# Second layer: four normalizations move from DVE to ACT, and POOL works out their shift

## The reference

```python
def _layernorm(x, axis=-1, eps=1e-05):
    m = jnp.mean(x, axis=axis, keepdims=True)
    v = jnp.var(x, axis=axis, keepdims=True)
    return (x - m) / jnp.sqrt(v + eps)

# _L1_xattn_ref, after the projections to 16 heads
scores = jnp.einsum('bhqd,bhkd->bhqk', q, k) * scale
attn = jax.nn.softmax(scores, axis=-1)
ctx = jnp.einsum('bhqk,bhkd->bhqd', attn, v)

x = x + _L1_xattn_ref(_layernorm(x), ctx_1024, ctx_1024, Wq, Wk, Wv, Wo)
x = x + _L1_ffn_ref(_layernorm(x), W, b, V_r, C)     # x @ W.T + b + (x @ V_r) @ C.T
```

## Time and profile before

| | us |
|---|---|
| median of three runs | 816.52 (815.5 to 820.49) |
| the profiled run | 817.38 |
| its span in the profile | 815.7 |
| busy: PE, DVE, POOL, ACT | 760.1, 474.5, 277.7, 264.3 |
| blocks 0 to 14 and the last batch | about 615 to 815.7 |

### The profile page before, as it was taken

How to read it: one execution, slowest core, us unless ns; L and a number is a source line. 1 busy time by engine, 2 the same in 40 slices (tenths; PEclk the granted TensorE clock), 3 DMA queues, 4 the chain that set the end, 5 groups by cost and what they waited for, 6 DMA issues and landing times.

```text
span 815.7 us, 14156 instructions
## 1 busy us (share of the span) xinstructions
PE 760.1 (93%) x5120; PEld 508.1 (62%) x5120; DVE 474.5 (58%) x1102; ACT 264.3 (32%) x524; POOL 277.7 (34%) x296
## 2 busy tenths in 40 slices
PE   6998999999999989989999999999989889999997
PEld 4675656755675555465666566555666666676775
DVE  2548564245734566814444473645658786888754
ACT  1323311241124121102222222222216665554562
POOL 4863615060320240611441433626693222101010
PEclk8999999999999999999999999999999999999999
DMA  9899434342250194844677654686767683662201
GB/s 257 225 307 324 123 104 131 115 133 76 87 176 15 28 375 172 278 126 125 185 201 206 194 177 140 183 251 172 214 178 203 171 224 114 182 182 71 73 2 46
DMA packets 70677, 133.53 MB, mean 164 GB/s; under 512 B 10401, under 2 KB 51362, under 8 KB 68690
## 3 DMA queue, kind: packets, MB, share of 16 engines
q1 hardware_dynamic: 54864, 81.14, 32.2%
q10 hardware_dynamic: 7906, 31.23, 13.9%
q0 software_dynamic: 7840, 20.26, 9.1%
HBM read 104.02 MB, written 28.41 MB: 162 GB/s over the span
## 4 chain that ended last, share of the span: by engine, by line
PE 74%; DVE 14%; ACT 4%; DMA 3%; issue 2%; POOL 1%; ACTq 0%; SPq 0%; DVEq 0%; POOLq 0%
PE ps L1323 14%; PE ps L1015 11%; PE ps L1339 7%; PE ps L1026 6%; PE ps L1036 4%; PE ps L2016 4%; DVE mxh L1662 4%; PE ps L2045 4%; PE ps L2036 3%; PE ps L2009 2%; PE ps L958 2%; PE ps L1330 2%; PE ps L1991 2%; PE ps L992 2%; PE ps L1046 2%
## 5 line engine op out<-in xcount | busy, mean ns | idle before, releaser
L1662 DVE TENSOR_REDUCE mxh<-ps 112x2 f32<-112x750 f32 x128 | 115.3, 934 | 22.9 <-PE ps L2016 21.5
L1323 PE MATMUL ps<-rw,rowsT 128*128 x280 | 126.1, 593 | 0.6 <-ACT rowsT L1282 0.6
L1875 ACT ACTIVATE d_pT<-ps 125x448 f32<-125x448 f32 x192 | 92.1, 548 | 66.9 <-PE ps L2036 63.5
L1015 PE MATMUL ps<-x1T,sw 128*128 128x448 f32 x256 | 102.8, 547 | 6.3 <-DVE gluT L465 4.9
L1323 PEld LDWEIGHTS ps<-rw,rowsT 128*128 128x128 f32 x280 | 50.5, 190 | 51.0 <-issue 51.0
L1015 PEld LDWEIGHTS ps<-x1T,sw 128*128 128x128 f32 x256 | 46.8, 190 | 51.7 <-issue 38.2
L2016 PE MATMUL ps<-kst,qst 96*112 96x375 bf16 x256 | 64.4, 339 | 7.8 <-DVE mxh L1662 2.8
L1339 PE MATMUL ps<-rw,gT 128*128 x280 | 66.4, 380 | 0.8 <-ACT gT L1286 0.8
L1339 PEld LDWEIGHTS ps<-rw,gT 128*128 128x128 f32 x280 | 52.9, 190 | 21.3 <-issue 15.9
L1026 PE MATMUL ps<-sw,gluT 128*112 128x256 f32 x256 | 57.8, 381 | 4.3 <-DVE gluT L465 4.3
L325 POOL DMA_INDIRECT xg<-xh_moe,places x32 | 32.8, 1024 | 83.4 <-DVE places L552 49.1
(11 more groups left out here) (239 smaller groups left out, 1257.2 us busy)
## 6 DMA issues: line engine op xcount, KB each, us to landing
rb<-in_rb SPq DMA_DIRECT2D x35, 512.0 KB, 4.3
kst<-kscr ACTq DMA_DIRECT2D x45, 378.0 KB, 5.2
rw<-in_rw SPq DMA_DIRECT2D x24, 512.0 KB, 9.9
kscr<-ka SPq DMA_DIRECT2D x16, 567.0 KB, 3.7
cT<-in_ctx_t SPq DMA_DIRECT2D x21, 378.0 KB, 5.0
ctxT<-in_ctx_t SPq DMA_DIRECT2D x16, 378.0 KB
ctxn<-in_ctx SPq DMA_DIRECT2D x16, 336.0 KB
qst<-qscr ACTq DMA_DIRECT2D x12, 448.0 KB, 6.8
```

Of the source, the lines that this page charges most:

```text
L1015: last = mm(bank[up_in(i, m)[k]][:, 0:GS], w[:, e, c, h * P:(h + 1) * P], x1T[:, c, :], start=c == 0, stop=c == C - 1)
L1323: last = mm(bank[1 + 2 * q + k], rowsT[:, q, c * P:(c + 1) * P], w[:, e, c, :], start=c == 0, stop=c == C - 1)
L1662: V.tensor_reduce(mxh[:, 2 * g:2 * g + 2], ps[0:S, p:p + 2, 0:K], axis=AX_X, op=ALU.max).then_inc(s["s_max"], 1)
L1875: A(pT[:, q % 2, k, :], bank[4 + k][0:KC, 0:QUAD * S], ACT.Exp).then_inc(s["p_ready"], 1)
```

## The change

In the four blocks of the table, DVE's four normalizing instructions go, and ACT makes the rows of `xh` as Identity(rstd * x + shift), with shift = -mean * rstd. One such instruction stands ahead of the exponentials of q = 2, one behind their first, one behind their third and one behind the first exponential of q = 3. ACT waits for the shift ahead of the first of them. POOL's part for these four, `rstd_and_shift`, has two instructions more than `rstd_of`, a product and a multiplication by -1, and one wait more, for the normalized rows of the group before. DVE waits for POOL's signal of the group before ahead of `mean_var` for "f" in the loop and after it. The norms beside the experts and the last group's "f" keep `normalized` on DVE and `rstd_of` on POOL.

```diff
+    def rstd_and_shift(pool, n, norm):
+
+        pool.wait_ge(s["xh_ready"], norm * G)
+        pool.wait_ge(s["mv_ready"], MV + norm + 1)
+        pool.tensor_scalar(rstd[:], mv[:, :, 1], EPS, None, ALU.add).then_inc(s["pool"], 1)
+        pool.wait_ge(s["pool"], n())
+        pool.tensor_tensor(rstd[:], rstd[:], mhalf[:], ALU.pow).then_inc(s["pool"], 1)
+        pool.wait_ge(s["pool"], n())
+        pool.tensor_tensor(shift[:], mv[:, :, 0], rstd[:], ALU.mult).then_inc(s["pool"], 1)
+        pool.wait_ge(s["pool"], n())
+        pool.tensor_scalar(shift[:], shift[:], -1.0, None, ALU.mult).then_inc(s["rstd_ready"], 1)
...
         combine(i)
-        rstd_of(pool, n, NORMS["q", i])
+        rstd_and_shift(pool, n, NORMS["q", i])
         split_queries(pool, i)
         split_rest(pool, i)
         for i in range(NG - 1):
-            rstd_of(pool, n, NORMS["f", i])
+            rstd_and_shift(pool, n, NORMS["f", i])
             add_bias(pool, i)
...
             if kind == "f":
                 v.wait_ge(s["x3_ready"], k * G + G)
+                v.wait_ge(s["rstd_ready"], MV + NORMS["f", k])
                 mean_var(v, n, k)
...
                 for g in range(2, 5):
                     maximum(b + 2, g)
-            if kind is not None:
-                normalized(v, k, NORMS[kind, k])
             if ahead_of:
                 maximum(b + 2, 5)
                 maximum(b + 2, 6)
...
         v.wait_ge(s["x3_ready"], i * G + AHEAD.stop)
+        v.wait_ge(s["rstd_ready"], MV + NORMS["f", i])
         mean_var(v, n, i, AHEAD)
...
+        def normalized(b, j):
+
+            if b in NORMALIZED:
+                kind, k = NORMALIZED[b]
+                if j == 0:
+                    a.wait_ge(s["rstd_ready"], MV + NORMS[kind, k] + 1)
+                A(xh[:, j, :], x_res[:, k * G + j, :], ACT.Identity, bias=shift[:, j:j + 1], scale=rstd[:, j:j + 1]).then_inc(s["xh_ready"], 1)
...
                 load_queries(a, b // G + 1)
+            normalized(b, 0)
             exps(b, 2, range(1))
             if what is not None:
                 turned_over(what, i)
+            normalized(b, 1)
             exps(b, 2, range(1, NKC))
+            normalized(b, 2)
             exps(b, 3, range(1))
+            normalized(b, 3)
```

More of the change, by code:

```diff
@@ L1369, in second_layer @@
     ((cT_1, cT_2, kst_1, vt, qst_1, kst_2, kst_3, va, pT, outT, heads, xhL, mxh, mr, mparts, mT, rec),
-     (wq1, wo1, wf, vrT, cfT, bf_b, identb, stat, mv, rstd, yg, xh, xhT, qa, qr, kst_0, qst_0, wv1, cT_0)) = tensors
+     (wq1, wo1, wf, vrT, cfT, bf_b, identb, stat, mv, rstd, shift, yg, xh, xhT, qa, qr, kst_0, qst_0, wv1, cT_0)) = tensors
     kst, qst, cT = (kst_0, kst_1, kst_2, kst_3), (qst_0, qst_1), (cT_1, cT_0, cT_2)
@@ L2297, in then @@
                 ("bf_b", [S, D], F32), ("identb", [P, P], BF16), ("d_stat", [S, G, 6], F32), ("d_mv", [S, G, 2], F32),
-                ("d_rstd", [S, G], F32), ("yg", [S, G, 2, D], F32), ("d_xh", [S, G, D], F32), ("d_xhT", [P, C, GS], F32),
+                ("d_rstd", [S, G], F32), ("d_shift", [S, G], F32), ("yg", [S, G, 2, D], F32), ("d_xh", [S, G, D], F32), ("d_xhT", [P, C, GS], F32),
                 ("qa", [P, 3, C, GS], BF16), ("qr", [P, C, GS], F32), ("kst_0", [P, NH, KP], BF16),
```

## The result

The changed kernel took 827.9 us (median of 7 runs, 823.52 to 828.39), the kernel before, run beside it, 818.84 (7 runs, 815.5 to 821.31). The ratio on record is 1.0095, with a 95% interval of 1.0064 to 1.0126: about 7.8 us slower, where 2.8 were forecast, and 827.9 lies above the range of 816.5 to 822.5. (The ratio is taken over the fast runs and isn't the quotient of the two medians, which lie 9.1 us apart.) A second comparison gave 1.0093 (1.0061 to 1.0125). Of the 8.6 us between forecast and result, 2.3 are the kernel before itself, whose median had been 816.52 with three runs; the rest is missing from the sum: 5.0 us by the ratio, 6.3 by the medians.

What follows compares the result with a forecast made beforehand. The prediction took TensorE, busy 93% of the span, to bound the kernel. It summed +3.9 (block 14) and -1.1 (blocks 4, 7, 11) to +2.8 us, taking the median from 816.52 to 819.3; range 816.5 to 822.5.

Steps and rivals of the forecast that it cites:

- Step 1: Blocks 4, 7, 11: without DVE's four instructions, scores could come 0.94 us earlier, at most 2.8 us; block 14 nothing.
- Steps 2 and 3: POOL's product 0.26 us and scaling 0.23 delay ACT's start; each normalizing instruction lasts 0.586, adding 0.48, an exponential 0.44.
- a load on that line: Sign that the forecast is wrong: an ACT function table load on line 1875 in the profile after.
- a dear product: Rival, chance 0.12: POOL's product costs as much as its power, 0.78 us later shift, +5.9 us, 822.4.
- a separate table: Rival, chance 0.02: Identity doesn't share the exponentials' set on ACT; 32 loads of 1.283, +41 us, about 858.
- Step 4: Blocks 4, 7, 11: fourth group's outputs come 0.37 us earlier each, 1.1 gained; the rest becomes a wait for ACT.
- Step 6: Edits priced at nothing: added POOL and DVE waits, POOL's bias addition starting about 706.4 instead of 704.84, ACT's key loads.
- The same step's other cover, the key loads: ACT's key loads at a block's end go out some 0.6 us later at no cost; cover thin by about 0.1.
- Step 5: Block 14: ACT's exponentials wait for POOL's shift; 3.9 us lost, about 2.0 late start and 1.9 the four instructions.
- not near 4: Sign that the forecast is right: in block 14 TensorE's waits for ACT's exponentials add up to near 4 us.
- an end that absorbs it: Rival, chance 0.10: TensorE runs the last batch later but no longer, absorbing block 14's delay; only -1.1 remains, 815.4.

Runs made afterwards that it cites:

- two_and_two: Changed kernel, block 14 back on DVE; elsewhere two normalizing instructions after group three's second exponential, two after the last, POOL's bias addition after DVE's small instructions; 0.9956 of kernel before.
- bias_later: Changed kernel, but POOL's bias addition in blocks 7 and 11 waits until DVE has made all four parts of the maxima; 1.0063 of the kernel before.
- before_collide: Kernel before, but POOL's bias addition in blocks 7 and 11 starts only after DVE's last maximum, over DVE's small instructions; ratio 1.0047.
- at_end: Changed kernel, but block 14 normalizes on DVE again and blocks 4, 7 and 11 have ACT's four behind the last exponential; 0.9996 of the kernel before.

## Why the prediction was wrong

**Step 1, what leaves DVE: right.** The wait of 0.94 us is gone, and two_and_two got back up to 1.11 us a block. **Steps 2 and 3, the prices: right.** The product was 0.20 (taken: 0.26), N0 started 0.65 us after the power's end (0.75), the four took 0.60 (0.586), and on ACT's timeline of block 14 each adds 0.49 and each exponential 0.43 (0.48 and 0.44). The product is even under the lower bound of 0.23. No new load of a table appears: each trace has nine, one of them at the second layer's first exponential (614.64 in both), so a load on that line alone would not have spoken against the forecast. The rivals of a dear product and of a separate table fall. That the first one's +5.9 is also what the trace of after gives is chance.

**Step 4: right where it stood alone.** Block 4, which adds no bias, gained 0.45 against 0.37, and so did block 11 once POOL's addition was moved (0.48). In block 7 of the changed kernel the fourth group's outputs came the same 0.45 earlier, and the loss lies behind them. The stall did turn into a shorter wait for ACT.

**Step 6 is the step that failed.** It priced POOL's later bias addition at nothing, since its readers come a block later. That is true of its readers; what I didn't ask is what DVE does while it runs. Before, the addition lay at 704.84 to 707.19, over DVE's maxima of 704.67 to 707.30. After, it starts 1.54 us later in the block, as step 6 said (706.4), while DVE, freed of four instructions, comes to its small ones 0.68 us earlier. So it lies over them, and one of them waits for its end: +1.94 us on DVE, and +1.10 and +0.90 at TensorE where -0.45 each was due, 2.9 us in all. bias_later takes 2.3 of these away and before_collide makes a like one, 1.71 a block, with nothing moved to ACT; so this is shown. The trace of before held the rows that tell it, in block 5, where POOL splits the queries:

```profile
680.59 1.89 POOL L1491 TENSOR_TENSOR qr<-qr,qa 128x896 f32<-128x896 f32 x1
...
680.67 1.83 DVE L1671 SCALAR_TENSOR_TENSOR mr<-mxh,mparts 112x16 f32<-112x16 f32 x1
```

A DVE instruction of 0.17 us takes 1.83 there and ends with POOL's. TensorE pays for it in the kernel before too: it waits 0.93 us for the parts of these maxima and 0.55 for the next maximum, as in before_collide (0.85 and 0.55). No run here moves POOL's work of block 5 away. The Trainium skill (SBUF — State Buffer, "SBUF: two separate sides") says that DVE and GpSimd share one pair of ports as an exclusive lock, held for a whole instruction, against DVE instructions in a two-port mode or, where the GpSimd one reads SBUF, with two SBUF inputs. The traces agree: two instructions with two SBUF inputs waited (2.23, 1.83), and the maxima from PSUM did not (0.93). The scaling of 2.11 has one SBUF input, and no trace shows in which mode it ran.

The same step's other cover, the key loads, was called thin by 0.1 us a block. In blocks 4 and 11 it held. In block 7 it gave way by about 0.6 us (bias_later: +0.15 in place of -0.45). There one load's issue took 1.00 to 1.86 us in each of the nine profiles in which ACT normalizes in block 7 (1.86 in the changed kernel, 1.32 in bias_later, 1.00 in at_end), where 0.6 is usual. In the changed kernel this hid behind the collision: block 7 lost only 0.2 us more than block 11, and the loss stayed 1.10 to 1.13 us with loads of 1.29 to 1.86. What the load waited for is open; before and before_collide, without ACT's normalizing in block 7, don't show it.

**Step 5: right in mechanism, short by the clock.** The late start of the exponentials was 2.2 us and cost 1.92 by itself (about 2.0 forecast); with the four instructions it comes to 3.84 (3.9 forecast). TensorE then ran at half clock behind its waits, which cost another 0.5 us in the profiled run and 2.2 in the second. That term was missing. TensorE's three waits add up to 3.17 us and not near 4; it is the lateness that fits. **The rival of an end that absorbs it falls:** the 4.36 us stand unchanged at the last batch's transposes.

**The sum** with the terms as measured: -0.45 + 1.10 + 0.90 + 3.84 = +5.4, plus 0.5 to 2.2 of clock, 5.9 to 7.7 us, against a timed 7.8 and 7.7 by the ratios. The forecast's +2.8 lacked the 2.9 us of the collision (with block 7's key load in it), of which 0.2 came back by blocks that gain 0.45 and not 0.37, and the clock. The range lacked them too: its bounds went through the prices of the new instructions, and none of those was the trouble. And a change of under 1% could be told from none: the interval is 0.3% to either side.

## What to carry to other kernels

Before moving work to another engine, look at where that engine's idle stretches lie and when the operand is ready: the same four instructions, with the wait for their operand, cost 3.84 us in front of exponentials that TensorE waits for and 0.94 behind them. They pay 0.74 to 1.11 us a block when they fill ACT's two gaps and POOL's addition is moved. When an instruction shifts in time, ask also what runs beside it: here a POOL instruction of 2.35 us on SBUF held up a DVE instruction of 0.17 us on SBUF until its end, and did not when it lay over maxima that DVE reads from PSUM. A place in the loop's last turns, where nothing covers ACT, needs its own answer.

## What the runs showed of the hardware

- POOL's price for a plain product of 112x4 is 0.20 us; the power of the same shape is 1.04.
- A POOL instruction of 2.35 us made one small DVE instruction on SBUF wait for its end (0.17 to 2.11, or 0.18 to 2.23).
- A wait of TensorE of 2.16 us in block 14, with two shorter ones behind it, went with a stretch at 1.2 GHz in each of the three profiles that have it; a wait of 1.67 us with one of 0.24 did not.
- Profiles of kernels that do the same up to block 4 stand +0.48 to +7.73 us there against before, and two of the changed kernel +2.54 and +7.73. Differences of a few us are better read between landmarks of two traces than from their spans.
